# A graph layer's search for each node's first edge: 16-bit block rows, 14 in flight, small batches of block numbers, later table rows

## The chip, the cores and the metric

The kernel runs on one core of one Trainium2 chip. The metric is the device time of one execution in microseconds; the time before is the median of three runs. Engines: PE (TensorE), DVE (VectorE), ACT (ScalarE), POOL (GpSimd), SP (SyncE).

## The reference

6250 nodes with 256 channels, 206250 edges (100000 random ones in both directions, and a loop per node), sorted by their destination `dst`. What is computed:

```
x = x + gat(layernorm(x), src, dst)
x = x + ffn(layernorm(x))

gat:  h = x @ W                      4 heads of 64
      a_src, a_dst = per-head dot products of h with att_src, att_dst
      dst' , src' = edges and once more a loop per node
      e = leaky_relu(a_src[src'] + a_dst[dst'], 0.2)
      alpha = softmax of e over the edges of one dst
      out = relu(segment_sum(alpha * h[src'], dst') + bias)
ffn:  30 times: h = h + 0.01 tanh(h); h = h * sigmoid(h)
                h = layernorm(h) * w + b; h = h @ W.T + b
```

## The kernel before

Partition p owns 49 nodes (NT) and 1612 consecutive edges (CW), so the work has three stages.

**Preparation** (up to 172 us). A table row of 264 floats per node (the four heads of h with a one behind each, and the four source logits) is made and stored in `haug`. The destination logits are scattered to `adz`, one row per edge, at the place of each node's first edge; reloading `adz` in edge order and filling it forward with a scan gives every edge its destination logit. So the kernel must know where each node's edges begin, and it searches for that in two steps:
- `dst` is loaded to `D` (L348, L349) and stored as 512 blocks of 403 values in DRAM, `dstp` (L351, 32-bit). The last value of each of the 512 blocks is broadcast to all partitions by PE (L834). For each of 50 columns of node numbers (NS = 50), ACT counts with Sign and an accumulator how many blocks end below the node (`count_blocks`, L410). DVE turns ten counts at a time into ten block numbers (`block_index`, L619).
- GpSimd fetches with an indirect DMA, for each partition, the block with that number (`find_row`, L524, "find" in what follows) into one of seven slots of a ring `LR` (RL = 7). DVE counts the values in it that are below the node (`count_edges`, L626). With the 50 counts a short chain (L671 to L687) makes the indices `begin_idx` for the scatters.

The order of the work around it is written out by hand. SP: D, the store of dstp, 18 loads of X, four stores of zeros to adz, copies of src, then seven stores of table rows (L371), adn (L374), the first index loads (L381), and the load of adz (L882) once the scatters are done. ACT: the 50 block counts, then per tile a copy of the transposed x (L417) and the logits (L423). GpSimd: 50 finds, a root (`root`, L532, the inverse square root of seven tiles' variances) behind finds 9, 16, 23, 30, 37, 44 and the last; then 49 scatters (L545), a gather `ad0` (L548), and the attention loop. PE: per tile two transposes (L846) and the projection (L854), at most four tiles ahead of the table rows. DVE: `block_index(0)`, the statistics of seven tiles, `block_index(1)`, and then one loop over t:

```
LAG = 18
for t in range(NT + LAG):
    if t < NS: count_edges(t)
    if t % 4 == 3 and 2 <= 1 + t // 4 < NS // SQ: block_index(1 + t // 4)
    if t + QT < NT: stats(t + QT)
    if t == NS - 1: (the chain that makes begin_idx)
    if t >= LAG: rows(t - LAG)
```

`rows(t)` (L649) scales the projection of tile t and writes its table row to `hrow`, which lies in the same stretch of SBUF as the ring. Behind that loop DVE makes KEEP and some other arrays (L691 to L727), then waits for adz and fills (L734).

**Attention loop** (172 to 2205 us). 124 steps of 13 edges per partition; GpSimd issues an indirect gather of table rows per edge column (L563), DVE and ACT work on them with scans (L747 to L804, L439 to L464), SP stores the sums.

**The rest** (to the end). The sums are merged, and the feed-forward part runs 30 times over all nodes on PE, ACT, DVE and GpSimd.

Of the kernel before, what the change touches and what calls it, by code (L numbers as in the profile page):

```python
# [4 lines left out]

F32 = mybir.dt.float32
I32 = mybir.dt.int32
U32 = mybir.dt.uint32
BF16 = mybir.dt.bfloat16
ALU = mybir.AluOpType  # L10
ACT = mybir.ActivationFunctionType
# [4 lines left out]
P = 128  # L16
# [7 lines left out]
ROW = SUMS + H  # L24


T = 13
STEPS = 124
CW = T * STEPS
# [11 lines left out]
SB = 403  # L41
NSB = EPAD // SB
assert NSB * SB == EPAD and NSB == 4 * P and CW == 4 * SB
NS = NT + 1
SQ = 10
assert NS % SQ == 0
RL = 7

QT = 7
NQ = NT // QT  # L50
# [102 lines left out]
def build(nc, x, src, dst, gW, att_src, att_dst, gbias, ln_w, ln_b, fW, fb, out):  # L153
    dram = dict(
        srcp=nc.dram_tensor("srcp", (EPAD,), U32).ap(),
        dstp=nc.dram_tensor("dstp", (NSB, SB), I32).ap(),
        haug=nc.dram_tensor("haug", (NODES, ROW), F32).ap(),
        adn=nc.dram_tensor("adn", (NODES, 2 * H), F32).ap(),
        adz=nc.dram_tensor("adz", (EPAD + NODES, H), F32).ap(),
        sums=nc.dram_tensor("sums", (EPAD + 1, ROW), F32).ap(),  # L160
    )
    with ExitStack() as ctx:
        sb = lambda name, shape, dt=F32: ctx.enter_context(nc.sbuf_tensor(name, shape, dt))
        sem = lambda name: ctx.enter_context(nc.semaphore(name))
        res = dict(
            ident=sb("ident", [P, P]),
            ones=sb("ones", [P, P]),
            X=sb("X", [P, NT, C]),
            half_neg=sb("half_neg", [P, NT]),
            bst=sb("bst", [P, NT, 6]),  # L170
            mv=sb("mv", [P, NT, 2]),
            ve=sb("ve", [P, NT]),
            rstd=sb("rstd", [P, NT]),
            nmr=sb("nmr", [P, NT]),
            adsum=sb("adsum", [P, NT, 2 * H]),
            eself=sb("eself", [P, NT, H]),
            end_idx=sb("end_idx", [P, NT], U32),
            e1_idx=sb("e1_idx", [P, 1], U32),
            maskneg=sb("maskneg", [P, P]),
            tail=sb("tail", [P, ROW]),  # L180
            WT=sb("WT", [P, 2, C]),
            b100=sb("b100", [P, C]),
        )
        attention(nc, sem, res, dram, x, src, dst, gW, att_src, att_dst, gbias, ln_w, ln_b, fW, fb)
        scan_ffn(nc, sem, res, dram, out)


def attention(nc, sem, res, dram, x, src, dst, gW, att_src, att_dst, gbias, ln_w, ln_b, fW, fb):
    ident, ones, X, mv, rstd, ve = (res[n] for n in ("ident", "ones", "X", "mv", "rstd", "ve"))
# [3 lines left out]
    srcp, dstp, haug, adn, adz, sums = (dram[n] for n in ("srcp", "dstp", "haug", "adn", "adz", "sums"))  # L193
# [3 lines left out]
    with ExitStack() as ctx:  # L197
# [3 lines left out]
        AD = sb("AD", [P, H, CW])  # L201
# [5 lines left out]
        assert R == 4  # L207
        early = G[:, 0:2, :, :].rearrange("p r t f -> p (r t f)")
        HROW = 2 * QT * ROW
        assert HROW + RL * SB <= 2 * T * ROW  # L210
        hrow = early[:, 0:HROW].rearrange("p (a t f) -> p a t f", a=2, t=QT)
        LR = early[:, HROW:HROW + RL * SB].bitcast(I32).rearrange("p (a c) -> p a c", a=RL)
        assert CW * H <= 2 * T * ROW
        raw = G[:, 2:4, :, :].rearrange("p r t f -> p (r t f)")[:, 0:CW * H].rearrange("p (c h) -> p c h", h=H)

        D = sb("D", [P, CW], I32)
        pads = sb("pads", [1, EPAD - E_IN], U32)
        nullrow = sb("nullrow", [1, ROW])
        iota_i = sb("iota_i", [P, P], I32)
        iota_k = sb("iota_k", [P, P])  # L220
        part_i = sb("part_i", [P, 1], I32)
        part = sb("part", [P, 1])
        nid_i = sb("nid_i", [P, NS], I32)
        nid = sb("nid", [P, NS])
# [3 lines left out]
        first = sb("first", [P, 1])  # L228
        first_idx = sb("first_idx", [P, 1], U32)
        tri = sb("tri", [P, P])  # L230
# [5 lines left out]
        sign1 = sb("sign1", [P, NS])  # L236
        cnt2 = sb("cnt2", [P, NS])
        cidx = sb("cidx", [P, NS], U32)
        begin = sb("begin", [P, NS])
# [34 lines left out]
        decay = sb("decay", [P, R, H])  # L274
# [9 lines left out]
        s_d = sem("s_d")  # L284
# [3 lines left out]
        s_zero = sem("s_zero")  # L288
        s_xpad = sem("s_xpad")
        s_iota = sem("s_iota")  # L290
        s_dstp = sem("s_dstp")
        s_misc = sem("s_misc")
        s_nid = sem("s_nid")
# [2 lines left out]
        s_cidx = sem("s_cidx")  # L296
        s_lr = [sem(f"s_lr{i}") for i in range(RL)]
        s_cnt1 = sem("s_cnt1")
# [46 lines left out]
        def sync_prepare(sp):  # L345
            sp.wait_ge(s_dpad, 1)
            for p0, p1 in ((0, 112), (112, P - 1)):
                sp.dma_start(D[p0:p1, :], dst[p0 * CW:p1 * CW].rearrange("(p c) -> p c", c=CW)).then_inc(s_d, 16)  # L348
            sp.dma_start(D[P - 1:P, 0:E_LAST], dst[(P - 1) * CW:E_IN].rearrange("(a c) -> a c", a=1)).then_inc(s_d, 16)  # L349
            sp.wait_ge(s_d, 48)  # L350
            sp.dma_start(dstp.rearrange("(p b) c -> p (b c)", p=P), D[:, :]).then_inc(s_dstp, 16)  # L351
            for b in range(NQ):
                if b == REST // QT:
                    sp.wait_ge(s_xpad, 1)
                for p0, p1, t0, t1, rows in node_rows(x, b):
                    sp.dma_start(X[p0:p1, t0:t1, :], rows).then_inc(s_x[b], 16)

            sp.wait_ge(s_zero, 1)
            for q in range(4):
                sp.dma_start(adz.rearrange("(p c) h -> p (c h)", p=P)[:, q * ZR:(q + 1) * ZR],  # L360
                             raw[:, 0:ZR // 4 + 1, :].rearrange("p c h -> p (c h)")[:, 0:ZR]).then_inc(s_adz0, 16)
            sp.wait_ge(s_pads, 1)
            even = E_IN // P * P
            sp.dma_start(srcp[0:even].rearrange("(p c) -> p c", p=P), src[0:even].rearrange("(p c) -> p c", p=P)).then_inc(s_misc, 16)
            sp.dma_start(srcp[even:E_IN].rearrange("(a c) -> a c", a=1), src[even:E_IN].rearrange("(a c) -> a c", a=1)).then_inc(s_misc, 16)
            sp.dma_start(srcp[E_IN:EPAD].rearrange("(a c) -> a c", a=1), pads[:, :]).then_inc(s_misc, 16)
            sp.dma_start(sums[EPAD:EPAD + 1, :], nullrow[:, :]).then_inc(s_misc, 16)

            for b in range(NQ):
                sp.wait_ge(s_hrow, (b + 1) * QT)  # L370
                sp.dma_start(haug.rearrange("(p i) c -> p i c", i=NT)[:, b * QT:(b + 1) * QT, :],  # L371
                             hrow[:, b % 2, :, :]).then_inc(s_hst[b % 2], 16)
            sp.wait_ge(s_adsum, NT)
            sp.dma_start(adn.rearrange("(p i) c -> p i c", i=NT), adsum[:, :, :]).then_inc(s_adn, 16)  # L374
            sp.wait_ge(s_misc, 16 * 4)
# [19 lines left out]
        def scalar_prepare(act):  # L395
# [24 lines left out]
            def logits(t):  # L420
                act.wait_ge(s_h, t + 1)
                act.wait_ge(s_rstd, t + 1)
                nc.scalar.activation(adsum[:, t, :], ps_h[t % HB][:, ROW:WID], ACT.Copy, scale=rstd[:, t:t + 1]).then_inc(s_adsum, 1)  # L423

            act.wait_ge(s_nid, 1)
            act.wait_ge(s_lastbc, 1)
            for i in range(NS):
# [71 lines left out]
        def gpsimd_prepare(pool):  # L499
            ch = Chain(pool, s_pprep)  # L500
            g = nc.gpsimd
            g.memset(D[96:P, E_LAST:CW], PAD_DST).then_inc(s_dpad, 1)
            pool.wait_ge(s_dpad, 1)
# [11 lines left out]
            ch.add(g.memset(half_neg[:, :], -0.5))  # L515

            def find_row(i):
                if i % SQ == 0:
                    pool.wait_ge(s_cidx, i // SQ + 1)
                if i == 0:  # L520
                    pool.wait_ge(s_dstp, 16)
                if i >= RL:
                    pool.wait_ge(s_cnt2, i - RL + 1)
                pool.indirect_dma_start(out=LR[:, i % RL, :], out_offset=None, in_=dstp[:, :],  # L524
                                        in_offset=bass.IndirectOffsetOnAxis(ap=cidx[:, i:i + 1], axis=0),
                                        ).then_inc(s_lr[i % RL], 16)
# [41 lines left out]
        def vector_prepare(dve):  # L568
            ch = Chain(dve, s_dprep)
            v = nc.vector  # L570
# [20 lines left out]
            for j in range(4):  # L591
                last = v.tensor_scalar(lastd[:, j, :], ident[:, :], lasts[:, j:j + 1], None, ALU.mult)
            last.then_inc(s_lastd, 1)
            v.tensor_copy(first_idx[:, :], first[:, :])

            dve.wait_ge(s_in, 16 * 4)
# [18 lines left out]
                            ALU.add).then_inc(s_w2, 1)  # L615

            def block_index(q):
                dve.wait_ge(s_cnt1, (q + 1) * SQ)
                v.tensor_scalar(cidx[:, q * SQ:(q + 1) * SQ], sign1[:, q * SQ:(q + 1) * SQ], 0.5, NSB / 2,  # L619
                                ALU.mult, ALU.add).then_inc(s_cidx, 1)  # L620

            def count_edges(i):
# [31 lines left out]
                last = v.scalar_tensor_tensor(out=W2c[:, k, :], in0=ps_b[:, 0:WID], scalar=-1.0 / C, in1=W2[:, k, :],  # L654
                                              op0=ALU.mult, op1=ALU.add)
            last.then_inc(s_center, 1)
            block_index(0)
            for t in range(QT):
                stats(t)
            block_index(1)  # L660
            LAG = 18
            for t in range(NT + LAG):
                if t < NS:
                    count_edges(t)
                if t % 4 == 3 and 2 <= 1 + t // 4 < NS // SQ:
                    block_index(1 + t // 4)
                if t + QT < NT:
                    stats(t + QT)
                if t == NS - 1:
# [711 lines left out]
```

## Time and profile before

| | us |
|---|---|
| median of three runs | 3978.47 |
| lowest, highest | 3975.29, 3980.11 |
| the profiled execution | 3976.35 |
| its span | 3974.5 |

The span is from the first to the last instruction of the profiled execution; all times in rows count from its start. In a row of the timeline the first number is the start, the second the duration, and in brackets stands how long the engine had been idle before it and what ended that. The queue of DMA issues that an engine drives is written SPq or ACTq. "Packets" are what DMA engines move in one piece.

### The profile page before, as it was taken

What the parts mean: (1) busy time and instruction counts of PE and PEld (TensorE: products, weight loads), DVE (VectorE), ACT (ScalarE), POOL (GpSimd) and SP (SyncE); (2) the same over time, 40 slices, a digit from 0 to 9 for tenths busy, and PEclk for the clock granted to TensorE, in tenths of its full rate; (3) what the DMA queues carried; (4) which work ended last, traced back from release to release, by engine and by line L of the source; (5) the groups of instructions that cost most, each with busy time, mean ns of one, the idle gap of its engine ahead of it and who ended that gap; (6) DMA issues with size and microseconds to landing.
All of it is one profiled execution on the core that took longest, in us unless ns stands there. A gap on an engine that the chain in (4) does not pass through costs nothing. (4 is left out here: it accounts for less than half of the span.)

```text
span 3974.5 us, 52549 instructions
## 1 busy us (share of the span) xinstructions
PE 1671.6 (42%) x9142; PEld 1461.2 (37%) x9142; DVE 3148.7 (79%) x7423; ACT 2508.0 (63%) x4438; POOL 3180.0 (80%) x3312
## 2 busy tenths in 40 slices
PE   4200000000000000000000039999999999999997
PEld 3200000000000000000000028888888888888886
DVE  7467777777777777777778579888888888888887
ACT  5145555555555555555556477777777777777775
POOL 6777777777777777777777489999999999999996
PEclk9655555555555555555555569999999999999998
DMA  8256666666666666666666410000000000000001
GB/s 263 95 184 220 218 219 210 219 215 215 214 219 218 221 219 205 223 217 215 215 215 231 162 50 1 0 0 0 0 0 0 0 0 0 0 0 0 0 0 65
DMA packets 127428, 491.37 MB, mean 124 GB/s; under 512 B 50089, under 2 KB 51370, under 8 KB 111332
## 3 DMA queue, kind: packets, MB, share of 16 engines
q0 software_dynamic: 84624, 235.32, 20.3%
q1 hardware_dynamic: 41188, 254.16, 17.0%
q10 hardware_dynamic: 1536, 1.18, 0.2%
q14 instruction: 74, 0.61, 0.0%
q8 instruction: 6, 0.10, 0.0%
HBM read 254.95 MB, written 236.40 MB: 124 GB/s over the span
## 5 line engine op out<-in xcount | busy, mean ns | idle before, releaser
L563 POOL DMA_INDIRECT G<-haug,idx x1612 | 1534.0, 952 | 497.7 <-issue 486.2
L1347 PE MATMUL ps_g<-WT,S 128*128 128x256 f32 x5880 | 1394.8, 380 | 0.0
L464 ACT ACTIVATE G<-RS 128x845 f32<-128x845 f32 x496 | 853.5, 1721 | 802.5 <-DVE RS L804 801.2
L1347 PEld LDWEIGHTS ps_g<-WT,S 128*128 128x128 f32 x5880 | 1060.0, 190 | 113.4
L804 DVE TENSOR_TENSOR_SCAN RS<-keep,psum 128x845 f32<-128x845 f32 x496 | 941.1, 1900 | 0.6 <-DVE z L747 0.4
L1063 POOL TENSOR_TENSOR S<-Hs,S 128x512 f32<-128x512 f32 (+1 forms) x750 | 938.3, 1251 | 3.4 <-ACT S L1134 3.2
L1323 PE MATMUL ps_x<-tdiag,ones 128*128 128x512 f32 x2 | 2.1, 1140 | 2092.4 <-DVE tdiag L1167 2092.4
L1276 DVE SCALAR_TENSOR_TENSOR Hs<-ps_g,r,b 128x256 f32 (+1 forms) x1470 | 682.8, 465 | 182.0 <-PE ps_g L1347 171.5
L1323 PEld LDWEIGHTS ps_x<-tdiag,ones 128*128 128x128 f32 x2 | 0.5, 309 | 2092.7 <-DVE tdiag L1167 2092.7
L1072 POOL TENSOR_TENSOR r<-cve,half_neg 128x2 f32<-128x2 f32 (+1 forms) x750 | 525.5, 701 | 147.0 <-DVE cve L1268 122.9
L1124 ACT ACTIVATE S<-ps_x 128x512 f32<-128x512 f32 (+1 forms) x750 | 441.4, 588 | 313.0 <-PE ps_x L1339 308.3
L1255 DVE BATCH_NORM_STATS2 cst<-S 128x6 f32<-128x256 f32 x1470 | 547.3, 412 | 9.8 <-issue 4.4
L1339 PE MATMUL ps_x<-ident,S 128*128 128x128 f32 x2940 | 445.4, 273 | 113.2 <-ACT S L1119 113.1
L1119 ACT ACTIVATE S<-S 128x512 f32<-128x512 f32 (+1 forms) x750 | 461.9, 616 | 33.5 <-POOL S L1063 26.0
L786 DVE TENSOR_TENSOR psum<-G,psum 128x845 f32<-128x845 f32 x496 | 477.4, 1030 | 2.1 <-ACT psum L448 2.1
L1134 ACT ACTIVATE S<-Hs 128x512 f32 (+2 forms) x750 | 461.0, 615 | 4.3
L1339 PEld LDWEIGHTS ps_x<-ident,S 128*128 128x128 f32 x2940 | 368.8, 141 | 190.3 <-ACT S L1119 114.6
L747 DVE TENSOR_TENSOR z<-G,AD 128x52 f32<-128x52 f32 x124 | 30.4, 245 | 466.0 <-DMA G<-haug,idx 463.0
L1268 DVE TENSOR_SCALAR cve<-cmv 128x2 f32<-128x2 f32 (+1 forms) x750 | 250.4, 334 | 1.1
L1262 DVE BATCH_NORM_AGGREGATE cmv<-cst 128x2 f32<-128x6 f32 x1470 | 175.4, 159 | 0.3
L459 ACT ACTIVATE carried<-RS,decay 128x65 f32<-128x65 f32 x492 | 153.7, 384 | 0.1
L448 ACT ACTIVATE psum<-el 128x56 f32<-128x56 f32 x124 | 27.6, 223 | 158.2 <-DVE el L777 158.2
(150 smaller groups left out, 1121.5 us busy)
## 6 DMA issues: line engine op xcount, KB each, us to landing
sums<-G SPq DMA_DIRECT2D x124, 1716.0 KB, 6.7
G<-haug,idx POOLq DMA_INDIRECT x1612, 2.9
haug<-G SPq DMA_DIRECT2D x7, 924.0 KB, 4.8
own<-haug SPq DMA_DIRECT2D x7, 924.0 KB, 4.7
X<-x SPq DMA_DIRECT2D x7, 784.0 KB, 25.4
out<-X SPq DMA_DIRECT2D x7, 784.0 KB
adz<-G SPq DMA_DIRECT2D x4, 830.5 KB, 37.0
G<-adz SPq DMA_DIRECT2D x1, 3224.0 KB, 11.2
```

What stands on the lines that cost most here:

```text
L464: nc.scalar.activation(G[:, k % R, :, h * HR:(h + 1) * HR].rearrange("p t f -> p f t"), RS[:, h, :, :], ACT.Copy).then_inc(s_rows, 1)
L563: pool.indirect_dma_start(out=G[:, u, t, :], out_offset=None, in_=haug[:, :], in_offset=bass.IndirectOffsetOnAxis(ap=idx[:, u, t:t + 1], a ...
L786: ch.add(v.tensor_tensor(ps_m[:, h, :, :].rearrange("p f t -> p t f"), G[:, u, :, h * HR:(h + 1) * HR], w, ALU.mult))
L804: v.tensor_tensor_scan(RS[:, h, :, :].rearrange("p f t -> p (f t)"), keep[:, k % 2, :, :].rearrange("p f t -> p (f t)"), ps_m[:, h, :, :]. ...
L1063: g.tensor_tensor(h1[:, u, 0:w * C], chunk_rows(Hs, j0 + u, w), th[:, u, 0:w * C], ALU.add).then_inc(s_add, 1)
L1072: g.tensor_tensor(r100[:, u, 0:w], cve[:, u, 0:w], half_neg[:, 0:w], ALU.pow).then_inc(s_r, 1)
L1119: nc.scalar.activation(h2[:, u, 0:w * C], h1[:, u, 0:w * C], ACT.Silu, scale=1.0 / HS).then_inc(s_silu, 1)
L1134: nc.scalar.activation(th[:, u, 0:w * C], chunk_rows(Hs, j0 + u, w), ACT.Tanh, scale=1.0 / HS).then_inc(s_tanh, 1)
L1255: last = v.bn_stats(cst[:, u, a, :], h2[:, u, a * C:(a + 1) * C])
L1276: ins = v.scalar_tensor_tensor(out=Hs[:, bass.ds(j * CH + a, 1), :].rearrange("p a c -> p (a c)"), in0=ps_g[u][:, a * C:(a + 1) * C], scal ...
L1339: last = nc.tensor.transpose(ps_x[XB[u]][:, n * P:(n + 1) * P], h2[:, u, n * P:(n + 1) * P], ident[:, :])
L1347: last = nc.tensor.matmul(ps_g[u][:, a * C:(a + 1) * C], h2T[:, u, (a * 2 + k) * P:(a * 2 + k + 1) * P], WT[:, k, :], start=(k == 0), stop ...
```

## The change

`dst` is converted to 16 bits on DVE (`D16`, in a part of the array AD that is not used yet) and dstp is stored, fetched and counted in 16 bits. The ring gets 14 slots in the same space. Block numbers are made in batches that end at 2, 5, 10, 15, ... 50; the first three ahead of the statistics, the one that starts at node column i0 behind count i0 - 6. ACT computes one Sign of one element ahead of its first wait. LAG goes from 18 to 40.

```diff
-        dstp=nc.dram_tensor("dstp", (NSB, SB), I32).ap(),
+        dstp=nc.dram_tensor("dstp", (NSB, SB), I16).ap(),
...
-SQ = 10
-assert NS % SQ == 0
-RL = 7
+
+BATCH = [0, 2, 5, *range(10, NS + 1, 5)]
+assert BATCH[-1] == NS
+RL = 14
...
+        D16 = AD[:, 0, 0:CW // 2].bitcast(I16)
...
-            sp.wait_ge(s_d, 48)
-            sp.dma_start(dstp.rearrange("(p b) c -> p (b c)", p=P), D[:, :]).then_inc(s_dstp, 16)
+            sp.wait_ge(s_d16, 1)
+            sp.dma_start(dstp.rearrange("(p b) c -> p (b c)", p=P), D16[:, :]).then_inc(s_dstp, 16)
...
+            act.wait_ge(s_iota, 1)
+            nc.scalar.activation(decay[:, 0, 0:1], ones[:, 0:1], ACT.Sign)
             act.wait_ge(s_nid, 1)
             act.wait_ge(s_lastbc, 1)
...
             def find_row(i):
-                if i % SQ == 0:
-                    pool.wait_ge(s_cidx, i // SQ + 1)
+                if i in BATCH:
+                    pool.wait_ge(s_cidx, BATCH.index(i) + 1)
...
             last.then_inc(s_lastd, 1)
+            v.tensor_copy(D16[:, :], D[:, :]).then_inc(s_d16, 1)
             v.tensor_copy(first_idx[:, :], first[:, :])
...
             def block_index(q):
-                dve.wait_ge(s_cnt1, (q + 1) * SQ)
-                v.tensor_scalar(cidx[:, q * SQ:(q + 1) * SQ], sign1[:, q * SQ:(q + 1) * SQ], 0.5, NSB / 2,
+                i0, i1 = BATCH[q], BATCH[q + 1]
+                dve.wait_ge(s_cnt1, i1)
+                v.tensor_scalar(cidx[:, i0:i1], sign1[:, i0:i1], 0.5, NSB / 2,
                                 ALU.mult, ALU.add).then_inc(s_cidx, 1)
...
-            block_index(0)
+            for q in range(3):
+                block_index(q)
             for t in range(QT):
                 stats(t)
-            block_index(1)
-            LAG = 18
+            LAG = 40
             for t in range(NT + LAG):
                 if t < NS:
                     count_edges(t)
-                if t % 4 == 3 and 2 <= 1 + t // 4 < NS // SQ:
-                    block_index(1 + t // 4)
+                if t + 6 in BATCH[3:-1]:
+                    block_index(BATCH.index(t + 6))
```

## Rows read from the trace of the kernel before

**Rows 1.** The page's costliest groups: busy us, mean ns | idle before, releaser.

```profile
L563 POOL DMA_INDIRECT G<-haug,idx x1612 | 1534.0, 952 | 497.7 <-issue 486.2
```

**Rows 2.** Windows: stretch, its length, engines' busy us, granted clock, DMA share, GB/s.

```profile
62.00:100.00 38.00, 33.55 (x152) 25.66 (x153) 37.54 (x141) 13.20 (x49) 29.73 (x30) 0.91 0.73 225
```

**Rows 3.** Timeline of GpSimd up to 240 us: start, duration, operation, idle before.

```profile
20.88 1.22 POOL L524 DMA_INDIRECT G<-dstp,cidx  x1 [13.72 <-DVE cidx L619]
...
31.67 0.94 POOL L524 DMA_INDIRECT G<-dstp,cidx  x1 [2.07 <-DVE junk L626]
...
60.70 0.95 POOL L524 DMA_INDIRECT G<-dstp,cidx  x1 [0.30 <-issue]
...
63.37 1.01 POOL L524 DMA_INDIRECT G<-dstp,cidx  x1 [0.18 <-issue]
...
100.00 0.96 POOL L524 DMA_INDIRECT G<-dstp,cidx  x1 [0.30 <-issue]
...
107.25 1.05 POOL L545 DMA_INDIRECT adz<-adsum,begin_idx  x1 [4.76 <-issue]
...
172.57 0.96 POOL L563 DMA_INDIRECT G<-haug,idx  x1 [0.30 <-issue]
```

**Rows 4.** Timeline of DVE: three of the 50 counts.

```profile
30.76 0.63 DVE L626 TENSOR_SCALAR_CACHE_REDUCE junk<-G,nid 128x403 bf16<-128x403 int32 x1 [3.49 <-DMA G<-dstp,cidx]
...
33.00 0.63 DVE L626 TENSOR_SCALAR_CACHE_REDUCE junk<-G,nid 128x403 bf16<-128x403 int32 x1 [1.26 <-DMA G<-dstp,cidx]
...
104.12 0.63 DVE L626 TENSOR_SCALAR_CACHE_REDUCE junk<-G,nid 128x403 bf16<-128x403 int32 x1 [0.30 <-DMA G<-dstp,cidx]
```

**Rows 5.** Timeline of 0 to 30 us: the way to the first find.

```profile
8.85 0.36 SPq L351 DMA_DIRECT2D dstp<-D  x1
...
9.12 0.87 DVE L592 TENSOR_SCALAR lastd<-ident,lasts 128x128 f32<-128x128 f32 x4
...
12.27 1.28 ACT L410 ACT_TABLE_LOAD   x1 [12.27 <-PE psum L834]
...
13.56 0.69 ACT L410 ACTIVATE junk<-psum,nid_half 128x512 bf16<-128x512 f32 x1
...
15.78 0.79 DVE L654 SCALAR_TENSOR_TENSOR RS<-psum,RS 128x272 f32<-128x272 f32 x2 [2.27 <-PE psum L837]
...
20.41 0.17 DVE L619 TENSOR_SCALAR cidx<-sign 128x10 uint32<-128x10 f32 x1 [3.84 <-ACT junk L410]
```

**Rows 6.** Timeline behind the scatters' start: long DVE operations, one issue beside them.

```profile
123.48 1.83 DVE L692 TENSOR_TENSOR KEEP<-D 128x1611 f32<-128x1611 int32 x1
...
125.23 1.89 DVE L693 TENSOR_SCALAR_CACHE_REDUCE ZC<-D,first 128x1612 bf16<-128x1612 int32 x1
...
127.16 1.05 DVE L695 TENSOR_SCALAR ZC<-KEEP 128x1612 f32<-128x1612 f32 x1
127.71 1.31 POOL L545 DMA_INDIRECT adz<-adsum,begin_idx  x1 [0.30 <-issue]
...
136.48 0.41 DVE L727 COPY b<-psum 128x256 f32<-128x256 f32 x1
```

**Rows 7.** From issue to landing: the last two X loads (L356), all finds (L524).

```profile
L356 SPq DMA_DIRECT2D X<-x x2: 386/406/427, 16.6 to 17.0; - x2
DMA to landing us min/median/max: 29.7/30.8/31.8
...
DMA to landing us min/median/max: 3.1/5.3/16.0
```

**Rows 8.** DMA queues of 28 to 46 us (two), of 300 to 2000 us.

```profile
q1 hardware_dynamic: 519, 2.93, 65.1%
q0 software_dynamic: 517, 1.67, 37.1%
...
q0 software_dynamic: 65251, 183.85, 37.0%
```

**Rows 9.** Timeline of DVE: a table row behind the begin chain.

```profile
110.13 0.49 DVE L649 SCALAR_TENSOR_TENSOR G<-psum,rstd,brow 128x264 f32<-128x264 f32 x1 [0.65 <-ACT adsum L423]
```

More of the change, by code:

```diff
@@ L7 @@
 I32 = mybir.dt.int32
+I16 = mybir.dt.int16
 U32 = mybir.dt.uint32
@@ L209, in attention @@
         HROW = 2 * QT * ROW
-        assert HROW + RL * SB <= 2 * T * ROW
+        assert HROW + RL * SB // 2 <= 2 * T * ROW
         hrow = early[:, 0:HROW].rearrange("p (a t f) -> p a t f", a=2, t=QT)
-        LR = early[:, HROW:HROW + RL * SB].bitcast(I32).rearrange("p (a c) -> p a c", a=RL)
+        LR = early[:, HROW:HROW + RL * SB // 2].bitcast(I16).rearrange("p (a c) -> p a c", a=RL)
         assert CW * H <= 2 * T * ROW
@@ L290, in attention @@
         s_iota = sem("s_iota")
+        s_d16 = sem("s_d16")
         s_dstp = sem("s_dstp")
```

## The prediction

> **What bounds the kernel now.** I read the page first. Its costliest group is the attention loop: L563 issues 1612 gathers, 952 ns busy each, and of the 497.7 us idle before them 486.2 are GpSimd's own issue gaps [rows 1]. That is 1.25 us per gather, one behind the other, so GpSimd sets the loop's length, and the loop starts when GpSimd is through its earlier work. What lies behind the loop waits for its last step and is not touched by the diff. So a microsecond won in GpSimd's part ahead of the loop is one of the total, until another start condition of the loop comes last. How loaded the rest is there: from 28 to 46 us the DMA engines are full, 65.1% for one queue and 37.1% for the other [rows 8]; from 62 to 100 us their share is 0.73, and DVE is busy 37.54 of the 38 us [rows 2].
>
> GpSimd's timeline gives the chain [rows 3]. The first find (a gather of one block of dst per node) starts at 20.88, having idled 13.72 us for cidx; the last starts at 100.00; the scatters of the logits start at 107.25, and 49 of them and the gather of ad0 end in the loop's first gather at 172.57. An undisturbed find takes 0.95 and a gap of 0.30, 1.255 in the long run. A root (L532) between two finds makes that 63.37 - 60.70 = 2.67, so 1.41 more. Without any wait, 50 finds with six roots among them take 1.22 + 0.30 + 48 x 1.255 + 6 x 1.41 = 70.2 us from first to last start. They took 79.12, so waits cost 8.9 us. They lie early: the eighth find, at 31.67, idled 2.07 [rows 3], since ring slot 0 must first be counted and its block is there only at 30.76 [rows 4].
>
> **Part 1, the start.** Find 0 needs block number 0 and dstp. Now numbers come in tens: ten sign counts on ACT behind a table load at 12.27 that waited for PE's L834, from 13.56 on and 0.66 apart, then cidx at 20.41, and GpSimd 0.47 later [rows 3, 5]. The first batch becomes two numbers, and the table load goes under ACT's idle time ahead of 12.27, so the second sign is done at 12.3 + 1.3 = 13.6 and the tenth at 18.9. Next in line is DVE: block_index stands behind W2c (15.78 + 0.79 = 16.57 [rows 5]), and the new cast of D sits ahead of that chain. No row shows this cast; bounds are L695, 1612 elements in 1.05, and L692, 1611 in 1.83 [rows 6]. It has one source and goes from SBUF to SBUF as L695, so I take 1.05: cidx at 17.6, find 0 at 18.1, 2.8 earlier (2.0 by the other bound). The dstp store was issued at 8.85; now it follows the cast (9.12 + 0.87 + 1.05 = 11.04 [rows 5]) with half the bytes, and has 7 us to land before it would come last. The 18 X loads, four zero fills and the src copies behind it on SP's queue move back 2.2 us with it. The last X load, issued at 17.0, landed 31.8 later, at 48.8 [rows 7]; it will be about 50.5. Its users are DVE's stats, needed for tile 42 only behind count 35, near 79 us, so this costs nothing.
>
> **Part 2, the blocks.** At 28 to 46 us the software queue moved 517 packets in 37.1% of 16 engines' time and the SP queue 519 in 65.1% [rows 8]: packet for packet, one each. Counts come 33.00 - 30.76 = 2.24 us apart there [rows 4], so 18 us hold 8 finds, 64 packets each: three of data and one small one per engine for its 8 rows of 1612 B. Engine time says the same: 64/517 x (0.371 + 0.651) x 18 = 2.28 us per find. The loop's gathers, rows of 1056 B, have 65251 packets for 1358 [rows 8], 48 each: two and one. For 806 B rows I take 48: the other queue's time per find falls by a quarter, 1.45 to 1.09, its own by nearly half, 0.83 to 0.46 (the small packets stay), together 1.55 us. The first block landed 9.9 us behind its issue; with a packet less 9.3. Bounds: 64 packets as now, 1.45 + 0.46 = 1.9; sharing by bytes, 0.73 + 0.41 = 1.14.
>
> The Trainium skill (DMA: Bandwidth & Descriptors, Queues, rings and completion order) says that an engine takes turns between its queues at packet granularity; by that rule alone, with the packets as many as now, a find would take the 1.9. The equal counts agree with it.
>
> **Part 3, the gate.** 14 slots lift the ring's wait, but block_index for node i0 stands behind count i0 - 6, so each batch of five waits for that count: five to ten are in flight where it was seven. From landing to the next find I take 1.05 us: the count 0.63, the number 0.17 [rows 4, 5], and the hand-overs. Landing i is at 27.4 + 1.55 i. Finds 0 to 9 run freely (29.7). Find 10 could go at 32.3, waits for landing 4 (33.6) and goes at 34.65: 2.35 lost. Find 15 could at 40.9, waits for landing 9 (41.35), goes at 42.4: 1.5 lost. Find 20 waits for landing 14 (49.1): 50.15 against 50.1. From there X is in, and landings are short: the median over all 50 finds is 5.3 us, the least 3.1 [rows 7], under the gate's 6 x 1.255 = 7.5. So waits are 3.9 instead of 8.9, and find 49 starts at 50.15 + 29 x 1.255 + 4 x 1.41 = 92.2, 7.8 earlier. The last count waited 0.30 for its block [rows 4]; with half the bytes I take 0.2 of it.
>
> **Part 4, table rows behind the counts.** LAG 40 takes 22 rows of h (L649, 0.49 [rows 9]) from between the counts. DVE was busy all through that stretch and is not any more; alone this gives nothing, since GpSimd sets the pace. PE now stops after four tiles, near 52, and restarts near 84. It stopped and restarted so before, at a mean granted clock of 0.91 over 62 to 100 (so mostly at 2.4 GHz), and DVE, busy 37.54 of 38 us, waited for no logits [rows 2]; the new pace is no faster. After the begin chain 40 rows are left instead of 18, 0.65 + 0.49 = 1.14 each [rows 9]: from 98.4 to 144 at most, and the work from KEEP to b100, 123.48 to 136.89 [rows 6], then ends near 157.5. Its cover are the scatters, up to 172.57 - 8 = 164.6; 7 us are left. Scatter t at 99.3 + 1.26 t needs the logits of tile t, some 13 ahead at the start and then 1.14 apart: no wait. The last haug store, behind row 48, must land before the loop: 144 + 5 does. adn, the index loads and the adz load on SP's queue come behind it and ahead of the same point.
>
> **Sum.** 2.8 + 5.0 + 0.2 = 8.0 us. The profiled execution took 3976.35 us (span 3974.5 and 1.85 around it), 2.1 under the median of the runs, 3978.47. It would take 3968.3 and the median 3970.4. A measurement of this kernel can tell 0.2%, 8 us, so the forecast stands on that line.
>
> **Rivals.**
> *No waits left.* If queues share by bytes, 1.14 lies under the pace and the finds never stop: last one at 88.3, a gain of 11.9, 3966.6. Against: the equal packet counts.
> *As many packets.* If 64 remain, landing 4 comes at 35.1, landing 9 at 44.7, landing 14 near 52.3; find 20 goes at 53.4, find 49 at 95.4: a gain of 4.8, 3973.7. For it: no row has 806 B rows.
> *The gate is the new wait (slower).* If block and count together take L, five finds last L - 1.255 instead of 6.3, where seven in flight gave L/7 each. At the first find's 9.9 throughout, eight batches lose 2.4 each: find 49 at 107.5, 3986.0. It decides from L = 9 on, all the way. For it: 2.07 idle on the ring [rows 3], 16.0 at most [rows 7]. Against: the median of 5.3, with twice the bytes.
> *Counts in a faster mode hold up GpSimd.* Beside L695, a DVE operation at twice the rate, an issue took 1.31 instead of 0.96 [rows 6]. Counts of 16-bit values could do this 50 times: 17 us, and at every second find 8, which gives 3978.5 or more. Against: L693, a count like this with both ends in SBUF, ran 1612 elements in 1.89, half as fast as L695 [rows 6].
> The Trainium skill (VectorE: DVE Perf Modes, Side-by-side) has one-source operations on 16-bit values in SBUF run at four elements per cycle; no row has such input. By itself a shorter count changes nothing here, as GpSimd comes last.
>
> **Chances.** Forecast 0.60, over and under the line nearly evenly (0.32 faster, 0.28 same); no waits 0.15, faster; as many packets 0.15, same; gate 0.05, slower; fast counts 0.05, 0.03 same and 0.02 slower. Faster 0.47, same 0.46, slower 0.07. The range takes in the first three, with the 1 to 2 us by which a median moves: 3965.5 to 3975.5.
>
> **What would show it.** Right: table load before 7, find 0 at 18.1, waits of GpSimd ahead of finds 10, 15 and hardly 20 and none after, 48 packets per find, find 49 at 92, scatters from 99, loop from 164.6, counts still at 0.63. Wrong: waits at every fifth find, finds over 1 us busy, rows that wait for logits between counts 44 and 49, or a loop whose first gather waits for SP's stores.

## The result and the profile after

| | before | after |
|---|---|---|
| median of 17 runs | 3976.25 | 3969.38 |
| lowest, highest | 3974.46, 3980.11 | 3967.29, 3970.48 |
| the profiled execution | 3976.35 | 3968.26 |
| its span | 3974.5 | 3966.4 |

The ratio is 0.9982 with a 95% interval of 0.9975 to 0.9988: the kernel is faster, by 6.9 us or 0.17%. That is just under the 0.2% which the prediction took as what a measurement can tell, and the interval has both sides of that line in it. The median was forecast at 3970.4.

The timeline of GpSimd in the kernel after, against [rows 3] (L530 is the find, L551 the scatter, L569 the loop's gather; columns as there):

```profile
17.54 1.22 POOL L530 DMA_INDIRECT G<-dstp,cidx  x1 [10.37 <-DVE cidx L627]
...
35.11 1.01 POOL L530 DMA_INDIRECT G<-dstp,cidx  x1 [3.54 <-DVE cidx L627]
...
43.61 0.95 POOL L530 DMA_INDIRECT G<-dstp,cidx  x1 [2.44 <-DVE cidx L627]
...
51.41 0.95 POOL L530 DMA_INDIRECT G<-dstp,cidx  x1 [0.32 <-DVE cidx L627]
...
93.77 0.96 POOL L530 DMA_INDIRECT G<-dstp,cidx  x1 [0.30 <-issue]
...
102.12 1.05 POOL L551 DMA_INDIRECT adz<-adsum,begin_idx  x1 [5.86 <-issue]
...
167.70 0.96 POOL L569 DMA_INDIRECT G<-haug,idx  x1 [0.30 <-issue]
```

The first find starts 3.34 us earlier. Then there are exactly two long waits, ahead of finds 10 and 15, both for a batch of block numbers; find 20 has none to speak of, and nothing after it waits. From first to last find it is 76.23 us, 6.0 over the 70.2 without waits, where it was 8.9. The last find is 6.2 us earlier, but the scatters only 5.1 and the loop 4.9. Forecast were the last find at 92.2, scatters from 99.3 and the loop from 164.6, so the loop starts 3.1 us later than forecast.

The start, timeline of the kernel after, against [rows 5]:

```profile
5.56 1.28 ACT L430 ACT_TABLE_LOAD   x1 [5.56 <-issue]
...
9.58 0.99 DVE L600 CAST AD<-D 128x1612 int16<-128x1612 int32 x1
...
10.61 0.36 SPq L355 DMA_DIRECT2D dstp<-AD  x1
...
17.07 0.23 DVE L627 TENSOR_SCALAR cidx<-sign 128x2 uint32<-128x2 f32 x2
```

The table load lies under idle time, the cast (AD is the array that holds D16) takes 0.99, and find 0 follows the number by 0.47 as before.

DVE's counts in the kernel after, against [rows 4]: the first, the tenth and the last.

```profile
26.84 0.63 DVE L634 TENSOR_SCALAR_CACHE_REDUCE junk<-G,nid 128x403 bf16<-128x403 int16 x1 [3.81 <-DMA G<-dstp,cidx]
...
42.62 0.63 DVE L634 TENSOR_SCALAR_CACHE_REDUCE junk<-G,nid 128x403 bf16<-128x403 int16 x1 [0.65 <-DMA G<-dstp,cidx]
...
98.99 0.63 DVE L634 TENSOR_SCALAR_CACHE_REDUCE junk<-G,nid 128x403 bf16<-128x403 int16 x1 [2.75 <-DMA G<-dstp,cidx]
```

The first block landed 9.3 us behind its issue, as forecast. The next nine counts take 15.78 us, 1.75 each, where two neighbours were 2.24 apart before (2.29 on average over the first eight counts, 30.76 to 46.82). A count of 16-bit values takes the same 0.63. And the last count waits 2.75 us for its block.

DMA queues of the kernel after at 28 to 46 us, against [rows 8] (packets, MB, share of 16 engines):

```profile
q1 hardware_dynamic: 543, 3.10, 74.4%
q0 software_dynamic: 510, 1.09, 28.1%
```

And the software queue over the whole span, on the page of the kernel before and on that of the kernel after:

```profile
q0 software_dynamic: 84624, 235.32, 20.3%
```

```profile
q0 software_dynamic: 83824, 230.16, 19.8%
```

That is 800 packets less for 50 finds: 16 each, one per engine, so 48 packets per find as assumed. The two queues still move nearly as many packets as each other, 543 and 510. The other queue's share rose, though: its packets took 0.744 x 18 x 16 / 543 = 0.395 us each on average, where they had 0.361, and 543 of them stand against 510. They were no larger (3.10 MB / 543 and 2.93 MB / 519 are 5.7 and 5.6 KB), and no run shows why they took longer. So a find costs 48/510 x (0.744 + 0.281) x 18 = 1.74 us, not 1.55.

### The profile page after: what moved, and what is told of

Its sections match the earlier page's. It is cut to its first block and busy times, and to the rows that moved or that the text cites. A ratio compares the mean times of both kernels' runs of the same rounds, so it can differ in the third digit from the quotient of the medians.

```text
span 3966.4 us, 52560 instructions
## 1 busy us (share of the span) xinstructions
PE 1671.9 (42%) x9142; PEld 1462.4 (37%) x9142; DVE 3152.8 (79%) x7430; ACT 2508.2 (63%) x4439; POOL 3181.2 (80%) x3312
## 5 line engine op out<-in xcount | busy, mean ns | idle before, releaser
L569 POOL DMA_INDIRECT G<-haug,idx x1612 | 1533.5, 951 | 494.9 <-issue 482.8
```

Of the source, the lines that this page charges most:

```text
L569: pool.indirect_dma_start(out=G[:, u, t, :], out_offset=None, in_=haug[:, :], in_offset=bass.IndirectOffsetOnAxis(ap=idx[:, u, t:t + 1], a ...
```

## The experiments

Each was compared first by its places on GpSimd's chain, since single executions differ by several us in the attention loop. From first to last gather it took 2027.2 us in the profiled run of the kernel after, 2030.4 before and 2027.6 to 2036.5 in the experiments on chips like it. The rows of this table are from chips on which the kernel before took 3976 to 3986 us; a slower chip is told of below. Every row is one profiled execution, and "total" is its time. Only the first two kernels and the last were run more often on such chips, so the other totals say little.

| kernel | find 0 | waits in the search | find 49 | scatters | loop starts | loop's length | total |
|---|---|---|---|---|---|---|---|
| before | 20.88 | 8.9 | 100.00 | 107.25 | 172.57 | 2030.4 | 3976.35 |
| after | 17.54 | 6.0 | 93.77 | 102.12 | 167.70 | 2027.2 | 3968.26 |
| start alone | 17.04 | 12.7 | 99.98 | 107.88 | 173.29 | 2033.3 | 3980.34 |
| 16 bits alone | 20.53 | 4.4 | 95.10 | 103.22 | 168.54 | 2028.0 | 3969.69 |
| after, LAG 18 | 17.56 | 5.9 | 93.62 | 101.79 | 167.19 | 2034.7 | 3975.83 |
| after, LAG 44 | 17.50 | 4.8 | 92.50 | 98.31 | 162.93 | 2027.6 | 3963.74 |
| after, 7 slots | 17.86 | 5.4 | 93.43 | 101.72 | 167.36 | 2035.2 | 3976.72 |
| after, earlier batches | 17.86 | 0.6 | 88.69 | 96.92 | 162.48 | 2033.2 | 3969.61 |
| after, X held back | 17.62 | 0.7 | 88.49 | 95.47 | 161.03 | 2036.5 | 3973.07 |
| all three edits | 17.38 | 0.5 | 88.10 | 93.86 | 159.41 | 2030.0 | 3962.57 |
| earlier batches, LAG 44 | 17.92 | 0.5 | 88.61 | 94.42 | 159.02 | 2028.1 | 3961.05 |

Waits are find 49 minus find 0 minus 70.2. "All three edits" are the earlier batches, X held back and LAG 44.

**The start alone.** My sum had counted 2.8 us for it.

```diff
-SQ = 10
+BATCH = [0, 2, 5, 10, 20, 30, 40, 50]
...
+            act.wait_ge(s_iota, 1)
+            nc.scalar.activation(decay[:, 0, 0:1], ones[:, 0:1], ACT.Sign)
             act.wait_ge(s_nid, 1)
...
-            block_index(0)
+            for q in range(3):
+                block_index(q)
             for t in range(QT):
                 stats(t)
-            block_index(1)
+            block_index(3)
```

> Kernel before with the small first batches and the early table load alone (32-bit blocks, seven slots, LAG 18). Theory A (blocks come at the rate at which the DMA engines take turns by packet, 2.24 us apart while X loads): find 0 at 17.1, its block 9.9 later, and the whole sequence moves with it, find 49 at 96.5 to 97.5 against 100.00. Theory B (the X loads' end at 48.8 sets when the finds run freely, whenever they start): find 49 at 99.5 to 100.

GpSimd's timeline of this kernel (L526 is the find):

```profile
17.04 1.22 POOL L526 DMA_INDIRECT G<-dstp,cidx  x1 [9.87 <-DVE cidx L622]
...
28.62 0.95 POOL L526 DMA_INDIRECT G<-dstp,cidx  x1 [2.83 <-DVE junk L629]
31.54 0.94 POOL L526 DMA_INDIRECT G<-dstp,cidx  x1 [1.97 <-DVE junk L629]
...
99.98 0.96 POOL L526 DMA_INDIRECT G<-dstp,cidx  x1 [0.30 <-issue]
```

Find 0 goes 3.84 us earlier, and find 49 0.02 earlier. What is won at the start comes back as waits for slots, 12.7 us instead of 8.9. So my theory A fell, and find 49 came where B had it: the blocks' landings decide here, and not the time at which the first find starts. They did not keep the pace that A assumed. The software queue moved 481 packets in 28 to 46 us, 7% fewer than the 517 of before, and the first nine counts were 2.48 us apart instead of 2.3 (27.71 to 47.52). Why the blocks came further apart this execution does not show, so B's reason, the end of the X loads, is not shown by it either.

**16 bits alone.**

```diff
-        dstp=nc.dram_tensor("dstp", (NSB, SB), I32).ap(),
+        dstp=nc.dram_tensor("dstp", (NSB, SB), I16).ap(),
...
+            v.tensor_copy(D16[:, :], D[:, :]).then_inc(s_d16, 1)
```

(The ring's seven slots, the batches of ten and LAG 18 stay.)

> Kernel before with 16-bit blocks alone (batches of ten, seven slots, LAG 18). Theory A (two data packets instead of three per engine and find): find 0 at 20.9, counts 1.5 to 1.8 us apart while X loads, 48 packets per find, find 49 at 93.5 to 95. Theory B (bytes are not what the finds wait for; only their number in flight is): counts 2.2 us apart as before, find 49 at 99 to 100.

Find 49 at 95.10, just outside the 93.5 to 95 expected: 4.9 of the 6.2 us that the whole change won there, and the waits fall to 4.4. All else in the change together is worth the other 1.3 us, though it starts find 0 3.0 us earlier. The DMA queues of this kernel at 28 to 46 us:

```profile
q1 hardware_dynamic: 567, 3.30, 73.8%
q0 software_dynamic: 543, 1.15, 27.5%
```

At 48 packets per find these are 11 blocks in 18 us, 1.6 us each, where it was 8.

**LAG 18 in the kernel after.**

```diff
-            LAG = 40
+            LAG = 18
```

> Kernel after with LAG back to 18. Theory A (GpSimd paces the search; DVE has time for the rows): finds 0 to 24 as in the kernel after, find 49 at 93.8 to 95. Theory B (the rows between the counts hold back the counts for which a batch waits): new waits of GpSimd between 55 and 95 us, find 49 at 97 or later. The last block lands 2.7 to 3.8 us after its issue, if no store of rows falls on it.

Find 49 at 93.62 and the scatters at 101.79: the rows between the counts cost GpSimd nothing. That one execution took 3975.83 us, though, with a loop of 2034.7 us. To see whether that belongs to the edit it was timed again, on a chip that turned out slower in every stage (before: 4233.95):

> Kernel after with LAG 18 again, timed. In one look its search and scatters were 0.5 us earlier than in the kernel after, but its attention loop took 2034.7 us from first to last gather where the kernel after took 2027.2. Theory A (the loop's length varies by several us between executions and has nothing to do with LAG): median within 1.5 us of the kernel after, ratio to before 0.9977 to 0.9987. Theory B (LAG 40 shortens the loop): ratio 0.9990 to 1.0005.

The ratio was 0.9984, interval 0.9975 to 0.9993, beside 0.9982 of the kernel after: LAG 18 or 40 makes no difference that these runs can tell. In the profile on that chip the search had two more waits, of 1.23 and 1.51 us for batches at 82.7 and 91.7, so there the gate bound late too. Whether that is the rows between the counts or the chip is open, since the kernel after was not run on it.

**LAG 44.** In the kernel after the last block landed late. The find's line in the kernel after, for the last find alone:

```profile
L530 POOL DMA_INDIRECT G<-dstp,cidx x1: 957/957/957, 93.8 to 93.8; - x1
DMA to landing us min/median/max: 5.2/5.2/5.2
```

And SP's timeline of the kernel after, the first store of table rows:

```profile
93.75 0.35 SPq L375 DMA_DIRECT2D haug<-G  x1
```

```diff
-            LAG = 40
+            LAG = 44
```

> Kernel after with LAG 44, so that the first store of seven table rows is issued behind the last count and not beside the last find. Theory A (that store holds up the last block, which landed 5.2 us after its issue where its neighbours took 2.7): landing 2.7, scatters from 99.6 instead of 102.12, loop from 165.2. Theory B (the 5.2 us are a load of instructions or chance): scatters from 102 as before, or other finds hit.

The last find's line in this kernel:

```profile
L530 POOL DMA_INDIRECT G<-dstp,cidx x1: 957/957/957, 92.5 to 92.5; - x1
DMA to landing us min/median/max: 2.7/2.7/2.7
```

And its timeline, the first scatter and the first store of table rows:

```profile
98.31 1.05 POOL L551 DMA_INDIRECT adz<-adsum,begin_idx  x1 [3.32 <-issue]
98.34 0.35 SPq L375 DMA_DIRECT2D haug<-G  x1
```

With LAG 40 the store of the first seven rows, 924 KB, is issued 0.02 us ahead of the last find. With LAG 44 it comes behind the last count; the block lands in 2.7 us, like its neighbours, and the scatters follow the last find by 5.8 us instead of 8.35. Of the 4.8 us at the loop 2.5 are this; 1.3 came in the search, whose two early waits were shorter in this execution (2.86 and 1.94), ahead of anything that LAG touches, and 1.0 in the scatters.

LAG 40 did not bring this collision in, though. With LAG 18 the store of the fourth seven rows stands behind count 45, and with LAG 40 the first store behind count 46. The kernel after with LAG 18 has at its last find:

```profile
DMA to landing us min/median/max: 5.0/5.0/5.0
```

```profile
93.97 0.32 SPq L375 DMA_DIRECT2D haug<-G  x1
```

Its scatters follow the last find by 8.17 us. With 16 bits alone it is the same: store 0.28 behind the last find, 5.0 to landing, scatters 8.12 behind. In the kernel before the store came 0.98 behind the last find, and the last count could start 4.12 behind it. So the collision belongs to any LAG that issues a store about count 45, and once GpSimd waits less it falls on the last find more fully. LAG 44 moves it away.

**Seven slots.**

```diff
-RL = 14
+RL = 7
...
```

> Kernel after with 7 slots instead of 14. Theory A (the batch gate of count i0 - 6 binds before 14 slots do, so the extra slots are idle): find 7 waits some 1.2 us for the first count, after that find 49 comes at 93.8 to 94.6, within 1 us of the kernel after. Theory B (what is in flight carries the gain): find 49 at 97 or later.

Finds 7, 8 and 9 wait 2.19, 0.67 and 0.47 us for slots, and the waits for batches shrink in return to 1.10 and 1.66. Find 49 comes at 93.43. The seven additional slots were worth nothing to the search behind this gate. The execution as a whole took 3976.72 us, as long as the kernel before on that chip (3976.47), with a loop of 2035.2. It was not timed again, so that its long loop is chance, as with LAG 18, is likely but not shown.

**Batches made five counts earlier.**

```diff
             for t in range(QT):
                 stats(t)
+            block_index(3)
...
-                if t + 6 in BATCH[3:-1]:
-                    block_index(BATCH.index(t + 6))
+                if t + 11 in BATCH[4:-1]:
+                    block_index(BATCH.index(t + 11))
```

> Kernel after with each batch of block numbers made five counts earlier (behind count i0 - 11, the batch of 10 ahead of the loop), so that 14 finds can be in flight. Theory A (the two waits of 3.5 and 2.4 us in the kernel after are the gate's, and blocks then come in at GpSimd's pace or as fast as the DMA engines allow): find 49 at 88 to 89.5, scatters at 96 to 97.5. Theory B (they are the DMA engines', full until X is in, as the early start alone showed, which moved find 0 by 3.8 us and find 49 not at all): find 15 goes earlier, others wait for slots, find 49 at 92 to 94.

No find waits any more, find 49 at 88.69, 5.1 us earlier, though landings still take up to 12.2 us. With up to 14 in flight they are hidden. Seven slots with these batches were not run, so this shows what the batches add to 14 slots, and not that they need them. This kernel too has its first store beside the last find, and the late count. Its timeline:

```profile
88.68 11.32 SPq L375 DMA_DIRECT2D haug<-G  x2
88.69 0.96 POOL L530 DMA_INDIRECT G<-dstp,cidx  x1 [0.30 <-issue]
...
93.79 0.63 DVE L634 TENSOR_SCALAR_CACHE_REDUCE junk<-G,nid 128x403 bf16<-128x403 int16 x1 [2.63 <-DMA G<-dstp,cidx]
```

**X held back.**

```diff
             for b in range(NQ):
                 if b == REST // QT:
                     sp.wait_ge(s_xpad, 1)
+                if b > 2:
+                    sp.wait_ge(s_cnt2, (b - 2) * QT)
```

> Kernel after with the loads of X from the fourth batch on held back on SP's queue until 7, 14, 21 and 28 blocks are counted. Theory A (the X loads are what makes a block take up to 13 us to land): no landing over 7 us behind the first ten finds, waits for batches gone or under 1 us in all, find 49 at 88 to 89.5, scatters at 96 to 97.5. Theory B (the statistics then wait for X, and with them the counts and batches): find 49 at 94 or later.

All finds of this kernel, and its queues at 28 to 46 us:

```profile
DMA to landing us min/median/max: 2.6/3.6/9.0
```

```profile
q1 hardware_dynamic: 296, 1.79, 35.6%
q0 software_dynamic: 500, 1.08, 24.6%
```

With the SP queue at 35.6% instead of 74.4% the median landing falls from 5.0 to 3.6 us, the gate of six counts is enough, and find 49 comes at 88.49. So the two waits had two halves, the X loads that made landings long and the gate that let too few be in flight; taking away either one removes both waits. Landings of up to 9.0 us remained, over the 7 expected, but no find waited for one. Here the first store is issued at 90.18, 1.7 behind the last find, whose block lands in 2.6 us; the scatters, at 95.47, follow it by 7.0.

**Together.** All three edits in one kernel, run once and then timed on the slower chip; and the earlier batches with LAG 44, without holding X back, timed on it and on another:

> Kernel after with the earlier batches, the held back X loads and LAG 44 together. Theory A: find 0 at 17.5, find 49 at 87.8 to 88.3 (no wait), its block 2.7 us later, scatters at 94, loop at 159, 8 to 9 us less than the kernel after. Theory B (the zero fills and src copies, now later, fall on the scatters, or the work behind the table rows comes last): loop at 163 or later.

> Kernel after with batches five counts earlier and LAG 44. Theory A (gate worth 5.1 us, store beside the last find 2.5): find 49 at 88.3 to 88.8, scatters at 94 to 94.5, loop at 159.5 to 160; 7.5 to 8 us under the kernel after, ratio to before 0.9960 to 0.9968. Theory B (gains ahead of the loop are partly lost in it): ratio 0.9970 or more.

> The kernel with all three edits (gate, paced X, LAG 44) again, timed. Theory A: as t2_gate11_lag44 within 1 us, since with 14 in flight the finds no longer wait for landings, ratio to before 0.9958 to 0.9968. Theory B (pacing X costs or gains on its own): more than 1.5 us apart from it.

> The kernel with earlier batches and LAG 44 once more, since the first timing fell on a chip on which the kernel before took 4234 us, its PE stretches ran at a lower mean clock and the scatters waited 13.7 us for logits. Theory A (that wait belongs to that chip): on a chip where before takes 3975 to 3980, scatters at 94 to 94.5, waits of scatters for logits under 4 us, loop at 159 to 160, total 14 to 16 us under before, 7 to 8 under the kernel after. Theory B (LAG 44 brings the logits too close to the scatters everywhere): waits of 5 us or more, loop at 162 or later.

| | median | before, same chip | ratio | 95% interval |
|---|---|---|---|---|
| earlier batches, LAG 44 | 4218.93 | 4233.95 | 0.9959 | 0.9946 to 0.9973 |
| and X held back | 4216.93 | 4233.95 | 0.9957 | 0.9943 to 0.9971 |
| earlier batches, LAG 44, second chip | 3960.76 | 3975.91 | 0.9961 | 0.9947 to 0.9974 |

On the second chip the version with earlier batches and LAG 44 is 15.2 us under before. The kernel after was not run there; its median, from a chip on which before took 3976.25, is 8.6 higher. Its loop starts at 159.02, 13.6 us earlier than before. With X held back as well the median is 2.0 us lower, which is more apart than the 1.5 of theory B; but each is a median of five, spread over 5.5 and 12.3 us, so these runs show no difference, nor that there is none. The single execution of all three edits was 6.8 us under the median of the kernel after, for 8 to 9 expected. On the slower chip the scatters of this version waited for logits. Its row there, and the one on the second chip (busy, mean ns | idle before, releasers):

```profile
L551 POOL DMA_INDIRECT adz<-adsum,begin_idx x49 | 47.8, 975 | 29.7 <-issue 15.9 <-ACT adsum L427 13.7
```

```profile
L551 POOL DMA_INDIRECT adz<-adsum,begin_idx x49 | 48.4, 987 | 18.0 <-issue 13.1 <-ACT adsum L427 3.7 <-DMA adz<-adsum,begin_idx 1.2
```

13.7 us against 3.7, of which the usual gaps are a part. From 94 to 130 us TensorE, which makes the projections that the logits are taken from, had a mean granted clock of 0.81 there and 1.00 on the second chip, and ACT stood idle twice for 5.8 us with no release that the trace shows. LAG 18 is not free of it on that chip: its scatters waited 7.8 us for logits, 6.75 of them at once. So a late LAG leaves less lead for a slow stretch; what makes the stretch slow was not tried.

## Why the prediction was right, point by point

The time (3969.38 for 3970.4) and the mechanism of the forecast held: waits ahead of finds 10 and 15, hardly one at 20, none after, 48 packets per find, counts still at 0.63, the loop's start set by GpSimd. That the time came so near is in part luck. The sum was 2.8 for the start, 5.0 for the waits and 0.2 for the last block, 8.0 us at the loop's start. Measured were 3.3, 2.9 and 1.1 lost, so 5.1 at the scatters and 4.9 at the loop. The medians differ by 6.9, and the other 2.0 come behind the loop's start, where nothing was forecast. And the 8.0 were taken from a median of three runs, 3978.47, which 17 runs put at 3976.25; taken from that one they would have given 3968.3.

*Part 1, the start.* Find 0 came at 17.54 for 18.1, the cast at 0.99 for 1.05. As a term of its own it fails: I added 2.8 us for an earlier first find to 5.0 for shorter waits. Alone the start is worth 0.02 us at find 49, and on top of the 16 bits it is, with the new batches, slots and LAG, worth 1.3. An earlier start counts only where the landings keep up. So the step that failed is the one that held the waits apart from the start; the 16 bits carry 4.9 of the 6.2 us.

*Part 2, the blocks.* The packets per find were right, the price was not: 1.74 to 1.75 us instead of 1.55. I had scaled the other queue's time by the number of turns alone, 1.09 us per find. It was 48/510 x 0.744 x 18 = 1.26, since its packets took 9% longer and came 543 to 510. That is the main reason why the term for the waits, 5.0 us, came out as 2.9.

*Part 3, the gate.* With 1.75, landings 4 and 9 come late enough for waits of 3.5 and 2.4 in place of 2.35 and 1.5 (the rows count the usual 0.3 in). Waits were 6.0 in all for 3.9, and find 49 at 93.77 for 92.2: 6.2 us won for 7.8. That the gate takes over from the ring, told as a fact of the code there, is what the two runs with 7 slots and with earlier batches show.

*The last count.* I took 0.2 us won from the smaller block. It was 1.1 us lost, because the first store of table rows is issued beside the last find. Part 4 had listed those stores only for their end, ahead of the loop. This is a collision on the critical chain that I had not looked for; with LAG 44 2.5 us more were won. It would have come with LAG 18 as well, where 8.17 us lie between the last find and the scatters.

*Part 4, table rows.* Right in that they give GpSimd nothing, and that KEEP to b100 stays covered: the last row came at 145.94 and b100 at 159.37, and DVE then waited 18.61 us for adz. The logits waited for were 3.4 us of idle at the scatters, none over 0.31, which is the usual gap.

*Behind the loop's start.* The loop's first gather was 4.9 us earlier, the fourteenth 6.2 (194.68 for 200.87), since four gathers fall on the scans of the fill in both kernels, at 3.1 us and more each instead of 0.95, and one more was through before them. Not forecast, and no more than where the issue happens to fall. The rest, up to 8.1 us between the two profiled executions and 6.9 between the medians, arises further on in the loop, and no run shows where. The loop's length in other executions varies by more than that.

*The rivals.* No waits left: not in this kernel, but in those with a looser gate or X held back; the 88.3 worked out for it was measured as 88.10 to 88.69. Their reason is another than the rival's, since packets were not shared by bytes. As many packets: refuted by the 800. Gate as the new wait: it is the wait, but not worse than the ring was. Faster counts: refuted, 0.63 as before and no find over 1.01 but the first. The chances, 0.47 for over and 0.46 for under 0.2%, were as undecided as the result, 0.17% with an interval of 0.12 to 0.25%.

## What to carry to other kernels

When a ring gets more slots, look at what else limits how far the producer may run ahead: here 14 slots did nothing for the search behind batches made six counts ahead; with batches made eleven counts ahead every wait was gone. A start that is brought forward is only worth something if what follows is not bound by a shared resource; measure it alone before adding it to a sum. And when a chain gets shorter or a step is moved, the large transfers around it meet other pieces of the chain: ask which small transfer they now fall beside. Here the store stayed about where it was in the order, the last find moved onto it, and four more tiles of LAG parted them.

## What the runs showed of the hardware

An indirect gather of 128 rows makes fewer packets when its rows are smaller: 64 for 1612 B rows, 48 for 806 B and for 1056 B. While X loaded, a block took 1.74 us of the DMA engines instead of 2.28, 24% less for half the bytes. By the shares of the two queues, 0.35 us of that is the block's own transfer, 0.83 to 0.48, and 0.19 the other queue's turns in between, 1.45 to 1.26: most of a block's price there is the transfer it takes turns with.

A block of 103 KB that lands in 2.7 us with no store beside it takes 5.0 to 5.2 us beside one store of 924 KB issued within 0.35 us of it, seen in five kernels.

An indirect DMA issue on GpSimd that takes 0.95 us by itself took 3.1 beside the scans of the fill on DVE.

An ACT operation placed ahead of its first wait pulled the table load from 12.27 to 5.56 us, under the time in which ACT idled.
